# Cross-attention scores on two row groups of the array, tails in fewer planner steps, and separate gates at the end of a decoder layer

## What is computed

```python
x = x + self_attention(layernorm(x))          # 16 heads of 64, 4 key/value heads, softmax over 1024 keys
x = x + cross_attention(layernorm(x), ctx)    # 16 heads of 16, softmax over 64 context rows, mask
x = x + routed_ffn(layernorm(x))              # pick a cluster and a tile by calibrated scores, small spline
```

```python
q = (query @ Wq + bq).reshape(b, sq, 16, 16).transpose(0, 2, 1, 3)
scores = jnp.einsum('bhid,bhjd->bhij', q, k) * 16 ** -0.5
scores = jnp.where(mask[:, None, None, :], -jnp.inf, scores)
attn = jax.nn.softmax(scores, axis=-1)
out = jnp.einsum('bhij,bhjd->bhid', attn, v)
```

## Time and profile before

| | us |
|---|---|
| median of 3 runs | 1819.47 (1817.64 to 1820.15) |
| the profiled execution | 1818.39, its span 1816.1 |
| TensorE busy | 1727.1 (95%) |
| VectorE busy | 1163.6 (64%) |
| ScalarE busy | 1143.8 (63%) |
| GpSimd busy | 892.8 (49%) |

### The profile page before, as it was taken

One profiled execution on the slowest core, in us unless ns is written; L12 is line 12 of the kernel. 1 busy time (PEld: TensorE's weight loads), 2 busy tenths in 40 slices (PEclk: granted clock), 3 DMA queues, 4 the chain that ended last, 5 costly groups with the idle time before them and its releaser, 6 DMA issues.

```text
span 1816.1 us, 27480 instructions
## 1 busy us (share of the span) xinstructions
PE 1727.1 (95%) x9160; PEld 831.3 (46%) x9160; DVE 1163.6 (64%) x2784; ACT 1143.8 (63%) x1554; POOL 892.8 (49%) x811
## 2 busy tenths in 40 slices
PE   6999999999999899999999999999999999999994
PEld 4444454454544344454444435445454444544352
DVE  6575538567476765747657576665756767385767
ACT  5577756666476765666566764676656677567652
POOL 2444454645544544546645364545645456444620
PEclk9999999999999999999999999999999999999997
DMA  4300000101200000010200000001020001000000
GB/s 146 74 13 1 1 13 1 36 1 24 48 1 13 1 24 1 1 36 1 58 13 1 13 1 24 1 1 36 1 59 1 2 1 24 13 1 1 1 12 12
DMA packets 97246, 32.39 MB, mean 18 GB/s; under 512 B 76753, under 2 KB 91217, under 8 KB 97105
## 3 DMA queue, kind: packets, MB, share of 16 engines
q1 hardware_dynamic: 97104, 30.64, 8.1%
HBM read 13.56 MB, written 4.19 MB: 10 GB/s over the span
## 4 chain that ended last, share of the span: by engine, by line
PE 79%; ACT 8%; DVE 7%; issue 4%; POOL 1%; DMA 0%; ACTq 0%; DVEq 0%; SPq 0%; POOLq 0%
PE attended L1387 22%; PE key_scores L1366 21%; PE misc L1295 7%; PE misc L1427 6%; PE max_scores L1344 6%; PE misc L1467 3%; PE misc L1397 3%; ACT relu L1770 2%; ACT probs L1779 2%; PE misc L1458 2%; PE misc L1531 1%; PE misc L1300 1%; DVE relu L2073 1%; PE misc L1520 1%; PE misc L1509 1%
## 5 line engine op out<-in xcount | busy, mean ns | idle before, releaser
L1779 ACT ACTIVATE probs<-key_scores 128x1024 f32<-128x1024 f32 x512 | 524.6, 1025 | 455.9 <-PE key_scores L1366 392.7
L2581 POOL TENSOR_TENSOR prob_sum<-prob_sum,probs 128x512 f32<-128x512 f32 x383 | 492.2, 1285 | 133.0 <-ACT probs L1779 108.8
L1387 PE MATMUL attended<-probs,values 128*64 128x512 f32 x2048 | 551.4, 617 | 0.1
L2073 DVE CUSTOM_DVE_ANT_0 relu<-max_scores,relu 128x512 f32<-128x512 f32 x508 | 330.2, 687 | 248.5 <-PE max_scores L1344 247.1
L1366 PE MATMUL key_scores<-q_high,k_chain 64*128 64x512 f32 x2048 | 457.9, 443 | 19.0 <-ACT probs L1779 17.5
L1366 PEld LDWEIGHTS key_scores<-q_high,k_chain 64*128 64x128 f32 x2048 | 191.6, 184 | 459.2 <-ACT probs L1779 226.8
L2095 DVE TENSOR_TENSOR running_sum<-running_sum,probs 128x512 f32<-128x512 f32 x384 | 266.3, 694 | 11.4 <-ACT probs L1779 4.3
L1770 ACT ACTIVATE relu<-max_scores 128x1024 f32<-128x1024 f32 x254 | 259.1, 1020 | 13.5 <-PE max_scores L1344 10.8
L2577 POOL TENSOR_TENSOR prob_sum<-probs 128x512 f32<-128x512 f32 x64 | 82.1, 1283 | 349.2 <-PE misc L1397 342.3
L1344 PE MATMUL max_scores<-k_max,q_high 64*128 64x512 f32 x1016 | 209.6, 408 | 11.9 <-DVE row_max L2073 10.7
L1366 PE MATMUL key_scores<-q_low,k_chain 64*128 64x512 f32 x1024 | 202.9, 392 | 0.0
(11 more groups left out here) (457 smaller groups left out, 1897.4 us busy)
## 6 DMA issues: line engine op xcount, KB each, us to landing
k_chain<-k_chain SPq DMA_DIRECT2D x32, 256.0 KB, 3.7
shift_row<-row_max SPq DMA_DIRECT2D x512, 0.5 KB, 2.0
buf_a<-in_x SPq DMA_DIRECT2D x8, 512.0 KB, 4.0
x_in<-in_x SPq DMA_DIRECT2D x7, 512.0 KB, 4.8
k_max<-k_max SPq DMA_DIRECT2D x14, 256.0 KB, 3.5
out_x<-buf_b SPq DMA_DIRECT2D x7, 512.0 KB, 3.2
heads_out<-in_qkv_wT SPq DMA_DIRECT2D x1, 1536.0 KB, 10.0
wo<-in_o_wT SPq DMA_DIRECT2D x1, 1024.0 KB, 6.3
```

Source lines behind the costliest of these rows:

```text
L1387: tensor.matmul(attended[head * HD:(head + 1) * HD, :], values_of(b, g // 2)[:, kt, g % 2 * HD:(g % 2 + 1) * HD], prob_slot(u, kt, head), ...
L1779: scalar.activation(probs[(u * KT + kt) % len(probs)][:, :, :], key_scores[:, :, :], ACT.Exp).then_inc(S["exp"])
L2073: vector.tensor_tensor_reduce(out=relu_of(u, i)[:, head, :], in0=max_area(u, i)[:, head, :], in1=relu_of(u, i)[:, head, :], scale=1.0, sca ...
L2581: gpsimd.tensor_tensor(prob_sum[1][:, :], prob_sum[1][:, :], probabilities, ALU.add).then_inc(S["prob_sum1"])
```

## The change

Five things change.

1. `scores2` now does two pieces in one call. Each of four matmuls has 64 rows (4 heads) and 256 columns. Bank 0 gets heads 0 to 3 of both tiles, bank 1 heads 4 to 7 of both. A call takes both misc banks; `soft2(n)` frees the first and `soft2(n + 1)` the second. `p2T` reads the columns in the new order.
2. The tail generator yields differently. New words: BANK (early, if a bank is free and fewer than two were taken in the step), FREE (early, needs no bank), BOTH (both banks free, none taken). Both q2 stand in one step, so do both `projected2`; `cal_b`, `cal_d` and `cal_e` stand together; `mag` stands behind the first `directions`.
3. A key or value projection is only begun if a misc bank is free; `heads` isn't placed until the `out_proj` of the chunk before is. ROOM is also open in every step after the last max matmul.
4. In the two halves at the end, `gate` and `intervals` get room of their own, and the first gate's exponential no longer waits for `compress`; `pick_h` does.
5. `SIGNALS` counts two updates for a call of `scores2`.

The diff, cut to its core:

```diff
-BOTH = "early, with both banks"
+BANK, BOTH, FREE = "early, with a bank", "early, with both banks", "early, without a bank"
@@ finish
     plan.put("inv", u)
     yield LATE
+    t = unit(u)[0]
+    while t and ("out_proj", t - 1, NT - 1) not in plan.seen:
+        yield LATE
     plan.put("heads", u)
@@ calibration
     plan.put("cal_a", j, which)
-    yield EARLY
+    yield FREE
     plan.put("cal_exp", j, which)
     yield LATE
     plan.put("cal_b", j, which)
-    yield LATE
     plan.put("cal_d", j, which)
@@ tail
     for m in range(KC):
         plan.put_in_bank("q2", j, m)
-        yield LATE
+    yield LATE
+    for m in range(KC):
         plan.put("q2_ev", j, m)
-        yield EARLY
+    yield BOTH
+
     count = KC * nt
-    for n in range(count + 2):
-        pair_done = n >= 3 and n % 2 == 1
-        if pair_done:
-            plan.put_in_bank("attended2", j, n - 3)
-        if n < count:
-            plan.put_in_bank("scores2", j, n)
-        if n == count:
-
-            yield EARLY
-        else:
-            yield ROOM if n < count else LATE
-        if pair_done:
-            plan.put("out2", j, n - 3)
-        if n > count:
-            break
-        if n < count:
-            plan.put("soft2", j, n)
-            yield EARLY
-            plan.put("exp2", j, n)
-        if n >= 1:
-            plan.put_in_bank("weights2T", j, n - 1)
-        yield LATE
-        if n >= 1:
-            plan.put("p2T", j, n - 1)
-        if n < count:
-            plan.put("normal2", j, n)
-        yield EARLY
-    yield EARLY
+    for n in range(0, count + 2, 2):
+        if n < count:
+            plan.put_in_both_banks("scores2", (j, n), (("soft2", "soft2", j, n), ("soft2", "soft2", j, n + 1)))
+            yield ROOM
+            plan.put("soft2", j, n)
+            yield BANK if n else EARLY
+            plan.put("exp2", j, n)
+        if n:
+            plan.put_in_bank("weights2T", j, n - 1)
+            yield LATE
+            plan.put("p2T", j, n - 1)
+        if n < count:
+            if not n:
+                yield LATE
+            plan.put("normal2", j, n)
+        if n:
+            yield BANK
+            plan.put_in_bank("attended2", j, n - 2)
+        if n < count:
+            yield ROOM
+            plan.put("soft2", j, n + 1)
+        else:
+            yield LATE
+        if n:
+            plan.put("out2", j, n - 2)
+        if n == count:
+            break
+        yield BANK
+        plan.put("exp2", j, n + 1)
+        plan.put_in_bank("weights2T", j, n)
+        yield LATE
+        plan.put("p2T", j, n)
+        plan.put("normal2", j, n + 1)
+        yield BOTH if n + 2 < count else BANK
+    yield BOTH
     for pair in range(nt // 2):
         plan.put_in_bank("projected2", j, pair)
+    for pair in range(nt // 2):
         yield LATE
         plan.put("x2", j, pair)
...
-    yield LATE
-    plan.put("mag", j)
     yield BOTH
     for pair in range(nt // 2):
         plan.put_in_both_banks("directions", (j, pair), [("y", "y", j, pair)] * 2)
         yield LATE if pair else ROOM
+        if not pair:
+            plan.put("mag", j)
         plan.put("y", j, pair)
@@ attention
         units.go_on_all(EARLY_R)
-        prepared = preps.go_on(0, EARLY_R)
+        prepared = plan.free_banks() and preps.go_on(0, EARLY_R)
...
+        background.go_on(0, FREE)
+        if plan.free_banks() and plan.taken - taken < 2:
+            background.go_on(0, BANK)
         if plan.free_banks() == 2 and plan.taken == taken:
             background.go_on(0, BOTH)
...
-        room = (step + MAX_AHEAD) % 2 == 0
+        room = (step + MAX_AHEAD) % 2 == 0 or step + MAX_AHEAD >= UNITS * KT
@@ scores2 on TensorE
-                pe.wait_ge(*freed("scores2", j, n))
+                (m, first), cols, half = tile_of(j, n), tiles_of(j) * P, HB // 2
+                for part in range(2):
+                    pe.wait_ge(*freed("scores2", j, n, n=part))
...
-                tensor.matmul(bank("scores2", j, n)[:, :], spaces[j].d[:, m * cols + i * P:m * cols + (i + 1) * P],
-                              k2_block[:, m, :, :].rearrange("p a b -> p (a b)"),
-                              start=True, stop=True).then_inc(S["scores2"])
+                for i in range(2):
+                    queries = slice(m * cols + (first + i) * P, m * cols + (first + i + 1) * P)
+                    for part in range(2):
+                        rows, heads = slice(part * HD, (part + 1) * HD), slice(part * half, (part + 1) * half)
+                        done = tensor.matmul(bank("scores2", j, n, n=part)[:, i * half * SC:(i + 1) * half * SC],
+                                             spaces[j].d[rows, queries],
+                                             k2_block[rows, m, heads, :].rearrange("p a b -> p (a b)"), start=True, stop=True)
+                        if i:
+                            done.then_inc(S["scores2"])
@@ cal_exp of the halves, on ScalarE
                         act.wait_ge(*after("route", "route", j))
-                        act.wait_ge(*after("compressed", "compress", j))
@@ pick_h of the halves, on VectorE
                 dve.wait_ge(*after("pick", "first_max_h", j, 0))
+                dve.wait_ge(*after("compressed", "compress", j))
@@ soft2 on VectorE
-                scores3 = bank("scores2", j, n)[:, :].rearrange("p (h k) -> p h k", h=HB)
-                dve.wait_ge(*after("scores2", "scores2", j, n))
+                pair, part = n - n % 2, n % 2
+                scores3 = bank("scores2", j, pair, n=part)[:, :].rearrange("p (h k) -> p h k", h=HB)
+                dve.wait_ge(*after("scores2", "scores2", j, pair))
```

More of the change, by code:

```diff
@@ L483, in tail @@
     plan.put("stats", j, 3)
-    yield EARLY
+    yield FREE
     plan.put("root", j)
-    for pair in range(nt // 2):
-        yield LATE
-        plan.put("gamma", j, pair)
-    for pair in range(nt // 2):
-        yield LATE
-        plan.put("x3", j, pair)
+    yield LATE
+    plan.put("gamma", j, 0)
+    yield LATE
+    plan.put("gamma", j, 1)
+    plan.put("x3", j, 0)
+    yield LATE
+    plan.put("x3", j, 1)
     plan.put("store", j)
@@ L928, in __init__ @@
         flat = self.c[:, :, :].rearrange("p a b -> p (a b)")
-        self.gate = flat[:, 0:words].rearrange("p (k i c) -> p k i c", k=8, i=nt)
+        if residual is None:
+            self.gate = flat[:, 0:words].rearrange("p (k i c) -> p k i c", k=8, i=nt)
+        else:
+            self.gate = new("gate", 8, nt * CL).rearrange("p k (i c) -> p k i c", i=nt)
         self.intervals = flat[:, words:2 * words].rearrange("p (n k) -> p n k", k=KNOTS)
+        if residual is not None:
+            self.intervals = new("intervals", nt * CL, KNOTS)
         self.picked_by = flat[:, 2 * words:3 * words].rearrange("p (i c t) -> p i c t", i=nt, c=CL)
@@ L1836, in p2T @@
                     act.wait_ge(*after("directions", "directions", j - 1, NT // 2 - 1))
-                scalar.activation(spaces[j].p2T[:, :, (i % 2) * P:(i % 2 + 1) * P],
-                                  bank("weights2T_h" if j >= FIRST_HALF else "weights2T", j, n)[:, :].rearrange("p (j n) -> p j n", j=4),
-                                  ACT.Copy).then_inc(S["p2T"])
+                if j >= FIRST_HALF:
+                    dst = spaces[j].p2T[:, :, (i % 2) * P:(i % 2 + 1) * P]
+                    src = bank("weights2T_h", j, n)[:, :].rearrange("p (j n) -> p j n", j=4)
+                else:
+                    part = n % 2
+                    dst = spaces[j].p2T[:, 2 * part:2 * part + 2, :].rearrange("p j (i n) -> p j i n", i=2)
+                    src = bank("weights2T", j, n)[:, :].rearrange("p (i j n) -> p j i n", i=2, j=2)
+                scalar.activation(dst, src, ACT.Copy).then_inc(S["p2T"])
             def out2(j, n):
```

5 lines of the change are left out of this document (removed), and 2 rows, old and new, of the table SIGNALS.

## The result

The changed kernel takes 1903.85 us (median of four runs, 1901.95 to 1905.02), the kernel before 1819.55 (1817.64 to 1820.15): a ratio of 1.0464, 95% interval 1.0446 to 1.0482. It is slower, as forecast, but by 84 us where 35 were forecast, and lies above both ranges (1825 to 1878, and 1803 to 1874). The profiled execution has a span of 1903.2 us.

A forecast was written before the change was run, and what follows sets the result against it. TensorE's work and in-order waits were taken to set the pace of the loop's 512 exponentials. 1818.4 - 31.4 + 63.5 + 5.0 - 1.3 = 1854.2, called 1854 us; own case 1825 to 1878, eight in ten 1803 to 1874.

The forecast's parts named there:

- Part 1: Scores2 by row groups of 64 rows: 0.95 us a call in place of 2.12, gain 31.4 us.
- Part 3: Rest of a tail: work in fewer steps costs 0, mag behind directions 5 us, bounds 0 and 12.
- Part 2: Scores2 holds both misc banks, so TensorE waits six times a tail for soft2's subtraction: cost 63.5 us.
- step 466: In chunk 6, weights2T(0) comes behind the query projection, which nearly covers its wait.
- Part 4: At the end, the first gate's exponential no longer waits for compress: gain 1.3 us, bounds 1.0 and 1.5.
- The first, banks free in time: Misc banks free in time, scores2's gain stands alone: 1786 us, about 1812 with a third of stalls; chance 0.21.
- The second and third: Row groups don't run side by side: 1876 us, chance 0.04. ScalarE's exponential cycle hides gain and stall: 1815 to 1822, 0.05.

The follow-up runs named there:

- e1: The changed kernel with scores2's four matmuls on all 128 rows instead of 64: 1931.31 us, ratio 1.0611 to the kernel before.
- e3: The changed kernel with soft2 placed late in even steps instead of odd ones: 1839.39 us, ratio 1.0105 to the kernel before.
- e9: The kernel before with the calibration of the change alone: 1840.25 us, ratio 1.0116.
- e13: The kernel before with one line of the change, pickT a step earlier, right behind pick_one: 1833.86 us, ratio 1.0083.
- e4: The kernel before with only the later part of the new tail (behind projected2), scores and soft2 as before: 1891.09 us, ratio 1.0385.
- e5: e3 with all of the tail's later part as in the kernel before: 1804.84 us, ratio 0.9923 to the kernel before.
- e6: e3 with the calibration alone as in the kernel before: 1802.94 us, ratio 0.9911 to the kernel before.
- e11: e3 with the knot sum late in odd steps, calibration still merged: 1821.25 us, ratio 1.0006 to the kernel before.
- e10: The changed kernel with the knot sum late in odd steps, calibration still merged: 1905.87 us, ratio 1.0478 to the kernel before.
- e12: e6 with pickT and mag also as in the kernel before: 1812.81 us, ratio 0.9961 to the kernel before.
- e8: The kernel before with the separate gates alone, without the wait for compress: 1819.54 us, ratio 1.0003.
- e7: e3 with pickT a step later and mag ahead of directions, as in the kernel before: 1810.62 us, ratio 0.9963 to the kernel before.
- e2: The changed kernel with take giving a stage the other free bank where soft2 read the one in turn: 1915.24 us, ratio 1.0525 to the kernel before.

## Why the forecast was right in direction and wrong in size

- **Part 1** held to the hundredth: 0.95 us a call, 3.09 a step. One check in the rivals is loose: the 4.7 us of stalls per tail at which gain and cost balance leaves out Part 3's 5 us; with them it is 4.0. e1 bears out that the halves overlap (its 1.93 against my 1.8 without overlap).
- **Part 2** held: 2.12 us for the stall of 1.95, 63.1 us in the 42 places for which 63.5 were forecast, and seven waits of 0.57 us, one in each tail, where I had called the wait nearly covered (step 466): 67.1 in 49. e3 took 64 us out by moving soft2 alone. My walk of the last tail met the order of the changed kernel step by step; in the first five tails some of the seven waits lie up to four steps later. Up to step 44 that last tail took 4.7 us more than before and the one ahead of it 4.6, and the other five, counted to step 48, 1.5 to 3.2 each: 22 us for seven, where my terms gave (63.5 - 31.4) = 32. So the waits are as forecast, their net cost by steps is somewhat less, and the mechanism (a bank handed out by plan order, and released in VectorE's order) is shown.
- **Part 3 is the step that failed.** "Merging the calibration's steps: 0, with 7 us either way", and nothing at all on the `yield LATE` ahead of pickT that the diff drops. Alone, on the kernel before, the first costs 21 us (e9), the second 15 (e13), all edits of the later part together 72 (e4). I had said that I couldn't order the short waits by hand; that was a reason for a wide bound, and I took a narrow one. In the changed kernel itself this step shows as 14.1 us more of waits for row maxima and 10.8 for pickT, and all of its half clock lies in this part's steps. What I'd have needed stood in the trace of before: GpSimd's 2.37 us chain between cal_d and cal_g, and its 0.62 us operation (L2657) between pick_one and pickT, are each followed by an engine that waits in order. mag was nearly right: 5 us taken, directions' wait for y grew by 7.1.
- **The clock was not in the sum.** I read that it was at 9 tenths or more all along, and took it as given. There were 47.6 us more at half clock, about 24 us of time, all in the steps of Part 3; none of Part 2's stalls, up to 2.0 us long, was followed by it, and e3, without them, has the same 51 us. With the clock's part taken off, the loop is 61 us longer against the 37 of my sum; that 24 us is, to within 3, the row maxima (14.1), pickT (10.8), what directions took beyond my 5 (2.1) and soft2 beyond my sum (3.6), less the q_low wait that went (4.1).
- **Part 4** had the right gain for the exponential (1.4 for 1.3), and the wrong neighbour: "VectorE works without a break behind it" is true, but its first operation grew by 0.93 us. 0.5 us came out.
- **Rivals.** The first, banks free in time, is what e5 and e6 build: 1803 to 1805 us with the later part kept right, inside the 1786 to 1812 given for it. The second and third are out by e1 and by the steps of 4.83 us.

What isn't settled: e9 and e13 add up to 35 us, e4 has 72. Half clock alone makes 22 us of the difference ((64.6 - 6.8 - 13.6) / 2); the other 14 may be the moves of mag and of the end, which weren't run by themselves. Parts 1 and 2 together on the old later part, the case that the sum would fit best, weren't run either. Nor was it shown why one gap of 2 us is followed by half clock and a like one isn't.

## What to carry to other kernels

Where engines run a written-out order, count for each moved step who waits in order for whom, and what fills the time between the producer and the consumer; a step's parity (here: which engine has filler work in it) was worth more here than the number of steps (e3, e11), unless a tail's end slips into the next chunk (e10, e12). An edit that "only merges steps" on an engine with a helper (here VectorE with GpSimd) needs that helper's whole chain as its bound. And where TensorE is above 90% busy, leave room for the clock: by the same estimate it took 24 us here, but over 14 of the changed orders (all but e8) anything from 0.2 (e10, 22 over 102) to 0.9 us (e7, 19 over 20) for each us of added gaps, so it widens the range and can't be a fixed term.

## What the runs showed of the hardware

- **A busy TensorE can fall to half clock behind single gaps of 1.6 to 3 us.** Across these kernels the time at half clock in the loop goes from 3.4 to 102 us, while TensorE is busy for 90% of the span or more. It doesn't follow the sum of the waits: e2 has 10.7 us less of gaps than the changed kernel and twice its half clock; and most gaps of 1.5 us and more are followed by none.
- **VectorE and GpSimd get in each other's way.** x3 (L2499 before, L2538 in e12) reads two operands in SBUF; 28 instructions of one form each. Least, median and greatest ns of one, kernel before and e12:

```profile
L2499 DVE SCALAR_TENSOR_TENSOR buf_b<-buf_b,rstd,buf_a x28: 472/478/1518, 445.1 to 1737.0; 128x256 f32<-128x256 f32 x28
```

```profile
L2538 DVE SCALAR_TENSOR_TENSOR buf_b<-buf_b,rstd,buf_a x28: 471/1481/1510, 446.1 to 1735.1; 128x256 f32<-128x256 f32 x28
```

The same instruction takes 0.47 or up to 1.5 us, as the plan lays it beside GpSimd's additions of 1.3 us or not. In e12, all 21 that began while a GpSimd operation was running ended 0.28 us behind its end; the other seven took 0.47. The Trainium skill, "SBUF — State Buffer", section "Who interferes with whom", says that a VectorE instruction with two SBUF inputs contends with a GpSimd instruction that reads SBUF, and that the later one is blocked for the whole of it. The rows agree. A step moved on VectorE has to be costed at both lengths, which I did for none.
- **Row groups pay at once and in full fp32.** Four rounds of two 64x256 matmuls in eight records take 0.95 us, on the full array 1.93. A change of shape shows as some 0.09 us: within a call the rounds start 0.215 us apart, and the PV products 0.306 behind the last round (1681.687 to 1681.993).
